# A fused adaLN block on one core: the gate's spread in rounded parts, and a new order around the end of batch 0's attention

## The reference

```python
mod = (silu(c) @ wmod).reshape(2, 6, 1, -1)
sa, ca, ga, sb, cb, gb = (mod[:, i] for i in range(6))
ga, gb = ((2 * (m >= 0) - 1) * maximum(abs(m), 0.25) for m in (ga, gb))
h = layernorm(x) * (1 + ca) + sa
x = x + ga * (h @ (weight * block_mask).T + bias)          # "attention"
h = layernorm(x) * (1 + cb) + sb
g = silu(lora_linear(h, w1, A1, B1)) * lora_linear(h, w3, A3, B3)
x = x + gb * lora_linear(g, w2, A2, B2)                    # hidden size 1376
# lora_linear(x, w, a, b) = x @ w.T + 2 * (x @ a.T) @ b.T, rank 16
```

## Time and profile before

| what | value |
|---|---|
| median of three runs | 249.31 us (249.19 to 249.68) |
| profiled execution, its own time | 249.18 us |
| its span, first to last instruction | 247.4 us |
| PE busy | 239.4 us, 97% of the span |
| DVE, ACT, POOL busy | 150.2, 94.6, 40.6 us |
| mean granted clock of TensorE | 0.999 of full speed |

### The profile page before, as it was taken

One profiled execution on the slowest core, in us unless ns is written; L12 is line 12 of the kernel. 1 busy time (PEld: TensorE's weight loads), 2 busy tenths in 40 slices (PEclk: granted clock), 3 DMA queues, 4 the chain that ended last, 5 costly groups with the idle time before them and its releaser, 6 DMA issues.

```text
span 247.4 us, 3423 instructions
## 1 busy us (share of the span) xinstructions
PE 239.4 (97%) x1205; PEld 187.3 (76%) x1205; DVE 150.2 (61%) x258; ACT 94.6 (38%) x174; POOL 40.6 (16%) x57
## 2 busy tenths in 40 slices
PE   7899899999999999999999999999999999999993
PEld 5567566777778888888888778888888888888772
DVE  2778699989989768855654514745454245424524
ACT  2365388957443231646456212113121212122210
POOL 2002477412101033033032000340000000000000
PEclk9999999999999999999999999999999999999999
DMA  5999999502242342231233550040000000000005
GB/s 132 367 400 389 389 404 388 172 28 85 96 132 71 86 120 53 86 124 44 87 115 65 46 33 0 17 153 3 0 1 0 0 3 0 0 0 3 0 0 170
DMA packets 14565, 26.37 MB, mean 107 GB/s; under 512 B 1618, under 2 KB 3538, under 8 KB 14420
## 3 DMA queue, kind: packets, MB, share of 16 engines
q1 hardware_dynamic: 14112, 26.01, 33.2%
q10 hardware_dynamic: 436, 0.15, 0.2%
HBM read 23.26 MB, written 2.10 MB: 103 GB/s over the span
## 4 chain that ended last, share of the span: by engine, by line
PE 84%; DVE 8%; DMA 2%; issue 1%; ACT 1%; POOL 0%; SPq 0%; DVEq 0%; POOLq 0%; ACTq 0%
PE up_a L1346 17%; PE up_b L1346 16%; PE acc L1372 8%; PE up_a L1355 8%; PE acc L1374 8%; PE acc L1373 8%; PE up_b L1355 8%; PE acc L1300 3%; DMA wa<-in_weight 2%; PE side L1328 2%; DVE stats L816 2%; PE side L1300 2%; DVE wa_lo L918 1%; DVE xt L1006 1%; PE side L1333 1%
## 5 line engine op out<-in xcount | busy, mean ns | idle before, releaser
L1095 DVE TENSOR_TENSOR g<-up_b,g 128x512 f32<-128x512 f32 (+1 forms) x22 | 15.2, 690 | 43.2 <-PE up_b L1355 43.2
L1372 PE MATMUL acc<-w_hi,g_hi 128*128 128x512 f32 (+1 forms) x88 | 34.9, 397 | 0.0
L1374 PE MATMUL acc<-w_hi,g_lo 128*128 128x512 f32 (+1 forms) x88 | 34.8, 395 | 0.0
L1373 PE MATMUL acc<-w_lo,g_hi 128*128 128x512 f32 (+1 forms) x88 | 34.7, 395 | 0.0
L791 ACT ACTIVATE g_hi<-g 128x512 fp32r<-128x512 f32 (+1 forms) x22 | 13.9, 632 | 51.2 <-DVE g L1095 51.2
L976 DVE SCALAR_TENSOR_TENSOR raw<-side,raw 128x512 f32<-128x512 f32 (+2 forms) x31 | 20.2, 677 | 19.1 <-PE side L1328 11.4
L722 ACT ACTIVATE w_hi<-raw 128x512 fp32r<-128x512 f32 (+2 forms) x33 | 20.3, 625 | 17.2 <-DVE raw L976 17.2
L781 ACT ACTIVATE g<-up_a 128x512 f32<-128x512 f32 (+1 forms) x22 | 13.1, 597 | 33.0 <-PE up_a L1355 33.0
L1346 PE MATMUL up_a<-ht_hi,w_hi 128*128 128x512 f32 (+1 forms) x88 | 24.7, 401 | 0.3 <-ACT w_hi L722 0.3
L1346 PE MATMUL up_b<-ht_hi,w_hi 128*128 128x512 f32 (+1 forms) x88 | 23.8, 393 | 0.0
L1355 PE MATMUL up_b<-ht_lo,w_hi 128*128 128x512 f32 (+1 forms) x88 | 23.8, 392 | 0.0
(11 more groups left out here) (162 smaller groups left out, 340.6 us busy)
## 6 DMA issues: line engine op xcount, KB each, us to landing
raw<-in_ffn SPq DMA_DIRECT2D x33, 256.0 KB, 2.7
xt<-in_x SPq DMA_DIRECT2D x8, 256.0 KB, 10.8
wmod_sb<-in_wmod SPq DMA_DIRECT2D x2, 1024.0 KB, 13.8
wmod_sb<-in_wmod SPq DMA_DIRECT2D x1, 2048.0 KB, 14.6
out<-xt SPq DMA_DIRECT2D x8, 256.0 KB, 2.5
mask_sb<-in_mask SPq DMA_DIRECT2D x4, 256.0 KB, 6.5
ca_sb<-in_wmod_ca SPq DMA_DIRECT2D x4, 256.0 KB, 6.4
wa<-in_weight SPq DMA_DIRECT2D x4, 256.0 KB, 6.7
```

Source lines behind the costliest of these rows:

```text
L1095: nc.vector.tensor_tensor(g[0:w], up_b[0:w], g[0:w], ALU.mult).then_inc(g_ready, 1)
L1372: nc.tensor.matmul(acc[t][:], hi, down_hi[j][0:w], start=(j == 0), stop=False)
L1373: nc.tensor.matmul(acc[t][:], hi, down_lo[j][0:w], start=False, stop=False)
L1374: last = nc.tensor.matmul(acc[t][:], lo, down_hi[j][0:w], start=False, stop=(j == HT - 1))
```

## The change

Four edits that hang together:

1. **Gate spread by rounded parts.** `silu_c` gets a third column, batch 0's c once more, so that the gate rows hold batch 0's gates twice. ACT rounds all gates (`gate_high`), DVE forms on the second copy the rest and on the others the rounded value (`gate_split`, in the space of b13[:, 0]), and PE's four spread products take float32r operands. `spread(0)` on POOL, which writes b13, now waits on `gate_spread`.
2. **POOL rounds LoRA pieces 0 and 1** (`lora_first`, a TENSOR_SCALAR by 1.0), between x_low(2) and x_low(3); ACT's two roundings go. x_low(1) moves ahead of the root, x_low(3) waits on `uv_ready`. SP issues the two pieces' loads one x tile earlier.
3. **DVE's order.** columns_sa ahead of masked_weight_low(1, 2); after the gates gate_split, lora_part(0), uv_split, masked_weight_low(1, 3), lora_part(1).
4. **PE's order.** attend(1, 2, 0, first) ahead of gate_rows(0); attend(1, 0, 0, last_two) ahead of attend(1, 3, 2, first); mod_rows_f and columns_f each one group of products later.

Before, the acc0 and acc1 rows stood behind the last acc2 and acc3 rows. The diff, cut to its core:

```diff
@@ gpsimd
+            def lora_first(n):
+                lo, hi = LORA_CUTS[n]
+                pool.wait_ge(lora_loaded[n], 16)
+                nc.gpsimd.tensor_scalar(parts[:, lo:hi], lora_place(n), 1.0, None, ALU.mult
+                                        ).then_inc(parts_high_by_pool, 1)
...
-                if j:
+                if j == 0:
+                    pool.wait_ge(gate_spread, 1)
+                else:
                     pool.wait_ge(merge_out, PIECE[j - 1, 1] + 1)
...
             x_low(0)
+            x_low(1)
             root(NORM_A[0], slice(0, T))
             pool.wait_ge(norm_cols_ready, 1)
-            for k in range(1, KT):
-                x_low(k)
+            x_low(2)
+            for n in range(LORA_POOL):
+                lora_first(n)
+            pool.wait_ge(uv_ready, 1)
+            x_low(3)
             spread(0)
@@ scalar
+            def gate_high():
+                act.wait_ge(gates_ready, 1)
+                nc.scalar.activation(gate_parts, gates_a[:], ACT.Copy).then_inc(gate_high_ready, 1)
...
             row_sum(0)
-            row_sum(1)
+            gate_high()
             uv_high()
             norm_rows_evacuate(0)
-            lora_high(0)
-            lora_high(1)
+            row_sum(1)
@@ vector
+            def gate_split():
+                dve.wait_ge(gate_high_ready, 1)
+                nc.vector.scalar_tensor_tensor(gate_parts, f32(gate_parts), const[:, KEEP_GATE:KEEP_GATE + 1],
+                                               gates_a[:], ALU.mult, ALU.add).then_inc(gate_parts_ready, 1)
...
             gates_of(0)
+            gate_split()
+            lora_part(0)
+            uv_split()
             masked_weight_low(1, 3)
-            uv_split()
-            lora_part(0)
             lora_part(1)
@@ tensor
             uv()
             attend(1, 0, 2, first)
+            attend(1, 2, 0, first)
             gate_rows(0)
-            attend(1, 2, 0, first)
...
             attend(1, 2, 2, first)
+            attend(1, 0, 0, last_two)
             attend(1, 3, 2, first)
-            for m in range(3):
-                attend(1, 0, m, last_two)
+            attend(1, 0, 1, last_two)
+            attend(1, 0, 2, last_two)
+            attend(1, 1, 0, last_two)
             mod_rows_f()
-            for m in range(3):
+            for m in range(1, 3):
                 attend(1, 1, m, last_two)
+            attend(1, 2, 0, last_two)
             columns_f()
```

More of the change, by code:

```diff
@@ L47 @@
 LORA_A = (1, 4)
+LORA_POOL = 2
 LORA_LATE = (2, 4)
@@ L220, in build @@
         gates_a = block_ones
+        gate_parts = b13[:, 0]
         mid = [wa[:, t] for t in range(T)] * B
@@ L257, in build @@
         parts_high_ready = sem("parts_high_ready")
+        parts_high_by_pool = sem("parts_high_by_pool")
         parts_ready = sem("parts_ready")
@@ L295, in build @@
         gates_ready = sem("gates_ready")
+        gate_high_ready = sem("gate_high_ready")
+        gate_parts_ready = sem("gate_parts_ready")
         gate_spread = sem("gate_spread")
         gate_copied = sem("gate_copied")
-        gate_row_loaded = [[sem(f"gate_row_loaded{n}_{b}") for b in range(B)] for n in range(2)]
+        gate_row_loaded = [[None, sem("gate_row_loaded0_1")], [sem(f"gate_row_loaded1_{b}") for b in range(B)]]
         summed = sem("summed")
@@ L456, in _ @@
             for t in range(T):
-                if t == 2:
+                if t == 1:
                     load_lora(0)
@@ L590, in _ @@
             act.wait_ge(silu_c_cleared, 1)
-            nc.scalar.activation(silu_c[:, :, 0:B], ct[:, 0:KT], ACT.Silu).then_inc(silu_c_ready, 1)
+            nc.scalar.activation(silu_c[:, :, 0:B + 1], ct[:, 0:KT], ACT.Silu).then_inc(silu_c_ready, 1)
             act.dma_start(ident[:], identity).then_inc(ident_loaded, 16)
@@ L944, in lora_part @@
                 keep = KEEP_A if n in LORA_A else KEEP_B
-                dve.wait_ge(parts_high_ready, n + 1)
+                if n < LORA_POOL:
+                    dve.wait_ge(parts_high_by_pool, n + 1)
+                else:
+                    dve.wait_ge(parts_high_ready, n + 1 - LORA_POOL)
                 dve.wait_ge(const_loaded, 16)
@@ L1034, in _ @@
             moment_a(0, 3)
+            columns_sa()
             masked_weight_low(1, 2)
             dve.wait_ge(const_loaded, 16)
+            nc.vector.tensor_copy(select[:], const[:, SELECT:SELECT + KT])
             nc.vector.tensor_copy(half_on[:], const[:, HALF_ON:HALF_ON + 2]).then_inc(half_on_ready, 1)
-            columns_sa()
             norm_parts(0)
@@ L1182, in columns_ca @@
                     pe.wait_ge(ca_ready, k)
-                nc.tensor.matmul(acc[2][:, k * B:(k + 1) * B], mod_rows[:, 0:P], ct[:, KT], start=True, stop=True
+                nc.tensor.matmul(acc[2][:, k * B:(k + 1) * B], mod_rows[:, 0:P], ct[:, KT, 0:B], start=True, stop=True
                                  ).then_inc(ca_cols_out, 1)
@@ L1267, in spread_gate @@
             def spread_gate():
-                pe.wait_ge(gates_ready, 1)
+                pe.wait_ge(gate_parts_ready, 1)
+                pe.wait_ge(half_on_ready, 1)
                 pe.wait_ge(norm_rows_ready, 1)
@@ L1273, in spread_gate @@
                     last = nc.tensor.matmul(up_b[:, q * P:(q + 1) * P],
-                                            const[:, SELECT + q:SELECT + q + 1].broadcast_to([P, P]),
-                                            gates_a[:], start=True, stop=True)
+                                            select[:, q:q + 1].broadcast_to([P, P]),
+                                            gate_parts, start=True, stop=True)
                 last.then_inc(gate_spread, 1)
@@ L1517, in launch_inputs @@
     for q in range(KT):
-        consts[q * QUAD, SELECT + q] = 1.0
+        consts[[q * QUAD, q * QUAD + B], SELECT + q] = 1.0
+        consts[q * QUAD + B, KEEP_GATE] = -1.0
     for t in range(T):
```

10 lines of the change are left out of this document (6 added, 4 removed).

## The result

The changed kernel took **249.93 us** (median of 20 executions, 249.28 to 251.33) against 249.26 for the kernel before (20 executions, 248.87 to 249.68): ratio 1.0031 [1.002, 1.0041], slower by 0.67 us. The prediction was 250.4.

A forecast was written before the change was run, and what follows sets the result against it. Bound until the transposes by DVE's chain from the first attn_gate and by PE's filling, both nearly tight. DVE +1.1, PE +1.05, the later counts: 249.31 + 1.1 = 250.4 us, range 248.6 to 251.0.

The forecast's parts named there:

- the sum of 1.1: Start of the transposes: DVE's chain +1.1 us, PE's filling +1.05, the later one counts.
- (a) to (c): On PE: uv starts 0.7 us earlier, spread product 0.5 shorter, gates' absolute value starts at 30.27 instead of 30.52.
- POOL's roundings, 0.8 and 1.6 us: On POOL behind x_low(2): one-input roundings of 256 and 640 columns, scaled from 1.27 us for 512 columns.
- the gates' product held to 31.35, gate_split until 32.9 to 33.2, uv_ready at 34.3: On DVE ahead of the first attn_gate: POOL's two roundings hold these instructions as its two-input rests do.
- rival C: POOL's roundings don't hold DVE, being short or letting go early; -1.1 to -0.4 us, middle 248.6; chance 0.20.
- x_low(3) gets in ahead of lora_part(1): POOL's x_low(3), waiting under the weight's rest, goes first and holds DVE's lora_part(1) until 36.0.
- Rival B: DVE's lora_part(1) goes ahead of POOL's x_low(3), first attn_gate at 35.8 as before; +0.3, 249.6 us; chance 0.20.
- A: Case as summed: roundings hold DVE, then x_low(3) holds lora_part(1); +1.1 us, range 249.9 to 251.0; chance 0.47.
- case D: PE's savings and short roundings of 0.6 and 1.2 us meet x_low(3) going first; +0.4, 249.7 us; chance 0.13.
- S at 36.9, 1.1 later: Start of the first attn_gate on DVE, which opens its chain to the transposes: 36.9 instead of 35.79.
- PE waits for S: PE waits over 1 us for the first attn_gate ahead of the acc0 product; a passed group of 0.47 remains behind.
- mod_rows_f one group later: On PE: ACT's last moment about 0.4 us later, with 0.4 of room on POOL; no term, up to 0.3.

The follow-up runs named there:

- e10: Kernel before with two moves alone: columns_sa ahead of masked_weight_low(1, 2), attend(1, 2, 0, first) ahead of gate_rows(0); 249.21 us.
- e11: Changed kernel with POOL's two roundings as two-input subtractions of a zero tile, plus a memset of the zeros; 250.08 us in one execution.
- e1: Changed kernel with one swap on POOL, spread(0) ahead of x_low(3); 249.42 us.
- e7: Changed kernel with attend(1, 0, 0, last_two) moved two groups earlier on PE, right behind attend_end(0); 252.18 us.
- e4: Changed kernel with ACT instead of POOL rounding LoRA pieces 0 and 1; 248.96 us, ratio 0.9986 to the kernel before.
- e5: Changed kernel with six unread products on PE ahead of the one that waits for the first attn_gate; 249.75 us.
- e9: Changed kernel with ACT rounding LoRA pieces 0 and 1, x_low(3) behind POOL's spread and adds, its PE user behind mod_rows_f, gate rows issued earlier; 248.77 us.
- e2: Changed kernel with attend(1, 0, 0, last_two) put back behind attend(1, 3, 2, first) on PE; 249.78 us.
- e3: Kernel before with the gate spread by rounded parts alone; 249.46 us, ratio 0.9999 to the kernel before.
- e8: Changed kernel with x_low(3) behind POOL's spread and adds, its PE user behind mod_rows_f, batch 1's gate rows issued earlier; 249.21 us.
- e6: Changed kernel run once more, unaltered, on another chip; 249.87 us, ratio 1.0037 to the kernel before.

## Why the prediction was right, and where it was not

The direction, the range and the place were right; the sum of 1.1 contained one step that didn't happen, and lacked two terms that did.

- *PE's savings (a) to (c).* Foreseen -0.7, -0.5 and half a product group. Measured: uv 26.73 for 27.71, of which 0.2 is the anchor; the spread product 0.63 for 1.13. Right, and worth nothing alone, as e10 shows.
- *POOL's roundings, 0.8 and 1.6 us.* Measured 1.00 and 1.81, near the upper bound taken from the steps of the earlier trace rows. The memset of the earlier trace rows was no guide. The prediction's estimate from the GPSIMD Engine Reference of the Trainium skill, 3.1, was 0.6 and 1.2; the page's best case of 1.8 cycles an element at 1.2 GHz makes 0.38 and 0.96, to which the estimate adds some 0.2 each without saying so. The trace bears neither out.
- *The step that failed: the gates' product held to 31.35, gate_split until 32.9 to 33.2, uv_ready at 34.3.* They took 0.29 and 0.35; uv_split was done at 33.26. Two things were otherwise. The product came 0.02 ahead of the first rounding, not 0.1 behind it (0.02 to 0.05 ahead in all seven profiles), so that the first rounding didn't hold it. And the second rounding held lora_part(0) for 0.46 us only, letting go with 1.3 us of its 1.81 left. The second decides: held until 33.2, lora_part(0) and uv_split would still have been done at about 34.2, near the predicted 34.3 (an estimate with the prediction's own 0.3 and 0.7). This was the condition of rival C, that a one-input instruction "lets go early". The prediction carried the hold of the two-input L520 over to an instruction that no row showed; e11 gives it two inputs and finds the hold, S 0.90 later and T 1.13. The Trainium skill, SBUF — State Buffer, "Who interferes with whom", says that the second to issue fully blocks for the other's whole length; for POOL's two-input instructions the traces agree (0.35 became 1.19 in e11, 0.87 became 1.92 here), for the one-input roundings they don't.
- *x_low(3) gets in ahead of lora_part(1).* Right: 1.92 us, 1.05 of it hold (e1: 0.87 without). Rival B is refuted. By this A's second half stands with C's first half: that is what case D's sum of +0.4 described in size, and the undisturbed executions lie there (249.67 against its 249.7), though D's own condition, roundings of 0.6 and 1.2, didn't hold.
- *S at 36.9, 1.1 later.* Measured +0.18 against the anchor. The 0.9 between is the hold that didn't come.
- *PE waits for S.* Foreseen over 1 us at the acc0 product, measured 1.41. What it costs by itself was taken as 0.47 of passed work. The **missing term** is the clock: in 9 of 32 executions of this kernel the mean granted clock is 0.992 or 0.993, and they take about 1.4 us longer (251.1 against 249.67). A stretch at 1.2 GHz like the one in e7's profile would make both. It lifts the median of the 20 from 249.67 to 249.93.
- *mod_rows_f one group later, the second missing term: no term, up to 0.3.* Measured 0.33 of DVE's waiting for columns_f and 0.16 in T - S.

That the predicted 250.4 lies only 0.5 from 249.93 is thus partly luck: 0.9 too much at S, 0.2 missing behind S and 0.3 in the clock. Shown: the hold by one- and two-input roundings (e4, e11), x_low(3)'s hold (e1), the clock's part in e7's profile, and, on one chip, that the low executions come with the wait (9 of 18 with 1.41 or 2.51 us, none of 22 with up to 0.85). Supported, but not shown: that filling the wait ends them (e5, without the changed kernel beside it). Argued only: that the low executions of the changed kernel have their stretch at the same place, since no profile caught one of them. Open: why one wait of 1.41 us brings it and the next does not.

## What to carry to other kernels

Before summing an edit's parts, look up the kind of instruction that holds the other engine: a two-input instruction of POOL next to one of DVE cost nearly a whole length (1.05 us here, of the 1.27 that a rest takes alone), a one-input one 0.46 us of 1.81. Look too at which of the two starts first. So put POOL's two-input work where DVE reads PSUM (in e1 x_low(3) took its 1.27 beside the attn_gates, and they their usual 0.7), and give short copies to an engine that idles (e9). A product moved ahead of its input's arrival bought nothing here (e2) and opened one long pause in dense work, which seems to cost the clock; shorten the pause, or try to fill it. And when executions differ in their beginning by more than the effect, count from an anchor behind that beginning.

## What the runs showed of the hardware

- The granted clock of PE after one pause in otherwise dense work: pauses up to 0.85 us, none of 63 executions low (e1, e2, e3, e4, e8, e9); 1.09 us, none of 11 (e10); 1.41 us, 9 of 32 (changed, e6); 2.51 us, 5 of 6 (e7), with 3.4 us at 1.2 GHz in the profile although PE worked without a pause by then.
- A rounding of 640 columns with one input took longer on POOL than with two (1.81 against 1.60), each beside DVE's instructions, and yet held DVE less (0.46 against 0.84, e11).
- The gates' product took 0.29 where it started 0.02 ahead of a one-input rounding of POOL, and 0.79 where it started 0.08 behind a two-input one (e11).
- POOL is held too: two L558 took 2.29 beside two DVE instructions with two SBUF inputs (e1, e8), 1.76 to 1.93 beside one (changed, e9), 1.19 undisturbed.
